# Window attention on one core: values' products in 64-row halves behind the scores, totals in the values' bank copied by ScalarE, TensorE's loop filled to whole fetch blocks

## The reference

```python
x = x + conv(_gn(x))
# conv: q, k, v = xh @ Wq, xh @ Wk, xh @ Wv ; split into 16 windows of 8 x 8
sim = einsum('bmhid,bmhjd->bmhij', q * scale, k) + pos_emb   # i, j: windows; m: place in the window
attn = softmax(sim)
o = einsum('bmhij,bmhjd->bmhid', attn, v) @ Wo + bo
```

## Time and profile before

| | us |
|---|---|
| median of 3 runs | 3674.86 (3674.0 to 3676.15) |
| the profiled execution | 3674.84 |
| its span in the profile | 3672.9 |
| TensorE busy | 3608.4 (98%) |
| VectorE busy | 3032.9 (83%) |
| ScalarE busy | 2940.0 (80%) |
| GpSimd busy | 2045.4 (56%) |

### The profile page before, as it was taken

One profiled execution on the slowest core, in us unless ns is written; L12 is line 12 of the kernel. 1 busy time (PEld: TensorE's weight loads), 2 busy tenths in 40 slices (PEclk: granted clock), 3 DMA queues, 4 the chain that ended last, 5 costly groups with the idle time before them and its releaser, 6 DMA issues.

```text
span 3672.9 us, 167555 instructions
## 1 busy us (share of the span) xinstructions
PE 3608.4 (98%) x67842; PEld 2625.2 (71%) x67842; DVE 3032.9 (83%) x5028; ACT 2940.0 (80%) x5377; POOL 2045.4 (56%) x3334
## 2 busy tenths in 40 slices
PE   5999999999999999999999999999999999999998
PEld 3777777777777777777777777777777777777776
DVE  6888888888888888888888888888888888888876
ACT  6888888888888888888888888888888888888874
POOL 4555555555555555555555555555555555555553
PEclk9999999999999999999999999999999999999999
DMA  4555555555555555555555555555555555555544
GB/s 95 139 144 136 146 144 142 137 145 143 141 138 150 142 137 143 145 143 137 143 146 144 136 145 144 144 134 145 143 145 135 145 142 145 136 146 143 141 126 117
DMA packets 252111, 513.67 MB, mean 140 GB/s; under 512 B 62672, under 2 KB 63120, under 8 KB 251536
## 3 DMA queue, kind: packets, MB, share of 16 engines
q1 hardware_dynamic: 250000, 504.35, 52.4%
q10 hardware_dynamic: 1536, 0.07, 0.0%
HBM read 118.31 MB, written 117.44 MB: 64 GB/s over the span
## 4 chain that ended last, share of the span: by engine, by line
PE 87%; issue 5%; POOL 3%; DVE 2%; ACT 1%; DMA 0%; POOLq 0%; SPq 0%; DVEq 0%; ACTq 0%
PE ps_out L327 18%; PE ps_q L327 16%; PE ps_k L327 16%; PE ps_v L327 14%; PE ps_o L370 13%; PE ps_s L358 10%; POOL sc L724 1%; ACT xn L484 1%; POOL xlo L732 1%; POOL newton L706 1%; DVE part L622 0%; POOL sc L737 0%; PE ps_tot L423 0%; DVE sc L651 0%; DVE pt_f L664 0%
## 5 line engine op out<-in xcount | busy, mean ns | idle before, releaser
L724 POOL TENSOR_TENSOR sc<-sc,mx 128x512 f32<-128x512 f32 x512 | 536.5, 1048 | 876.3 <-DVE mx L658 876.3
L484 ACT ACTIVATE xn<-x_sb,norm_add,norm_mul 112x128 f32<-112x128 f32 x2048 | 1016.7, 599 | 5.0 <-POOL norm_add L717 3.1
L737 POOL TENSOR_TENSOR sc<-sc,rs 128x512 f32<-128x512 f32 x512 | 536.4, 1048 | 421.7 <-DVE rs L678 421.6
L327 PE MATMUL ps_out<-ohi,wo_s 128*112 128x256 f16 x4096 | 720.8, 278 | 3.1 <-DVE x_sb L634 3.1
L646 DVE TENSOR_TENSOR olo<-ps_o,ohi 128x512 f16<-128x512 f32 x512 | 353.8, 691 | 350.0 <-ACT ohi L526 338.8
L511 ACT ACTIVATE sc<-sc 128x512 f32<-128x512 f32 x512 | 323.3, 632 | 396.3 <-POOL sc L724 396.1
L327 PE MATMUL ps_q<-xhi,wqk 112*128 112x512 f16 x2048 | 611.2, 380 | 12.5 <-POOL xlo L732 9.9
L327 PE MATMUL ps_k<-xhi,wqk 112*128 112x512 f16 x2048 | 609.7, 379 | 0.6 <-ACT q_sb L501 0.6
L370 PE MATMUL ps_o<-p_bd,v_sb 128*32 128x128 f32 x16384 | 553.5, 276 | 9.1 <-DMA p_bd<-pt_f 6.6
L327 PE MATMUL ps_v<-wv_s,xhi 112*128 112x224 f16 x4096 | 560.6, 259 | 0.0
L732 POOL TENSOR_TENSOR xlo<-xn,xhi 112x1024 f16<-112x1024 f32 x256 | 547.3, 2138 | 13.1 <-ACT xhi L495 13.1
(11 more groups left out here) (76 smaller groups left out, 5827.6 us busy)
## 6 DMA issues: line engine op xcount, KB each, us to landing
k_bd<-k_cut SPq DMA_DIRECT2D x1024, 128.0 KB
p_bd<-pt_f SPq DMA_DIRECT2D x2048, 64.0 KB, 2.5
x_sb<-in_x SPq DMA_DIRECT2D x256, 448.0 KB, 4.5
out_y<-x_sb SPq DMA_DIRECT2D x256, 448.0 KB, 3.5
k_cut<-in_L_conv_Wq SPq DMA_DIRECT2D x2, 98.0 KB
k_cut<-in_L_conv_Wk SPq DMA_DIRECT2D x2, 98.0 KB
k_cut<-in_L_conv_Wv SPq DMA_DIRECT2D x2, 98.0 KB
pt_f<-in_L_conv_Wo SPq DMA_DIRECT2D x8, 24.5 KB
```

The lines of the kernel that those rows point to most:

```text
L327: last = nc.tensor.matmul(dst, w_parts(a, ch), x_parts(c, ch), start=(n == 0), stop=(n == 3 * chunks - 1))
L484: nc.scalar.activation(xn[:, b % 2, :, c4, :, :, nw].rearrange("p r c q -> p q r c"), x_sb[:, b % XBUFS].rearrange("p ch (nh r w) -> p (ch ...
L724: nc.gpsimd.tensor_tensor(rows, rows, mx[:, t % 2].unsqueeze(2).broadcast_to(by_row), ALU.subtract).then_inc(shifted, 1)
L737: nc.gpsimd.tensor_tensor(rows, rows, rs[:, t % 2].unsqueeze(2).broadcast_to(by_row), ALU.mult).then_inc(probs, 1)
```

## The change

Seven things:

1. `weigh_values` makes 64 matmuls in place of 32: each takes 64 rows (half of the tokens) and 64 moving columns. The halves write different banks; ps_o has two banks now, laid out by place, unit and window, so an output is four runs of 16 columns, 128 columns apart. p_bd is half as wide. `in_x_order`, by which ohi and olo read ps_o, has a step of 128 columns over both banks where it was 16 in one.
2. The waits of the values' products move up to those of the scores, ahead of the last k matmul, and the products follow the scores with nothing between.
3. ps_tot has no bank of its own: it lies in the v projection's bank behind the values' columns. Its matmul moves from the end of the step to between the q and v projections of the next one (TOT_LEAD 12 to 11; the join stays where it was, as JOIN_LEAD 12).
4. ScalarE copies and scales the totals into st (`keep_means`), between keeping q and keeping v. VectorE's operation that did so is gone, STAT_OPS is 6.
5. VectorE's six remaining operations of the statistics stand in one run after the residual add.
6. In each step the first 3, 3 or 2 q matmuls after the first are cut in two of 256 columns, by `cut(t)`, 64 matmuls more in a round.
7. TensorE's loop starts at slot 66 of a fetch block of 256 instructions (`head_slot`).

```diff
-LOAD_LEAD, SUM_LEAD, RSQ_LEAD, TOT_LEAD, STAT_LEAD = 15, 14, 13, 12, 11
+LOAD_LEAD, SUM_LEAD, RSQ_LEAD, JOIN_LEAD, TOT_LEAD, STAT_LEAD = 15, 14, 13, 12, 11, 11
...
-        p_bd = sb("p_bd", [128, 2, PAIRS, UNIT * 32])
+        p_bd = sb("p_bd", [128, 2, 2, UNIT * 32])
...
-        ps_o = ps("ps_o", [128, UNIT * 32])
-        ps_tot = ps("ps_tot", [128, 2 * G])
+        ps_o = ps("ps_o", [128, 2, 512])
+
+        ps_tot = ps_v[0:CP, 0, C:C + 2 * G]
...
+        def cut(t):
+
+
+            return (3, 3, 2)[t % 3]
+
...
-            return ap.rearrange("p (u c n) -> p u n c", u=T2 * HG, n=WIN)
+
+            return ap.rearrange("p a (c u n) -> p u n (a c)", c=WS // 2, n=WIN)[:, 0:T2 * HG]
...
-                        last = nc.tensor.matmul(dst, w_parts(a, ch), x_parts(c, ch),
-                                                start=(n == 0), stop=(n == 3 * chunks - 1))
+                        for cols in (slice(0, HTOK // 2), slice(HTOK // 2, HTOK)) if 0 < n <= in_two else (slice(None),):
+                            last = nc.tensor.matmul(dst[:, cols], w_parts(a, ch), x_parts(c, ch)[:, cols],
+                                                    start=(n == 0), stop=(n == 3 * chunks - 1))
...
+            def total(b, i):
+                if b is None:
+                    return
+                per_image(pe, joined, b, i)
+                per_image(pe, means, b - 1, i)
+                nc.tensor.matmul(ps_tot, ones[0:CP, 0:CP], both[:, b % 2], start=True, stop=True).then_inc(totals, 1)
...
-                        for h in range(HPG):
-                            unit = (((h // 2) * T2 + t2) * HG + hg) * 2 + h % 2
-                            col = (t2 * HG + hg) * 128
-                            last = nc.tensor.matmul(
-                                ps_o[h * 32:h * 32 + 32, col:col + 128].rearrange("p (r j) -> p r j", j=32),
-                                v_sb[:, g % VBUFS, t2, hg * HPG + h, :],
-                                p_bd[:, g % 2, :, unit * 32:unit * 32 + 32], start=True, stop=True)
+                        for half in range(2):
+                            rows = slice(half * 64, half * 64 + 64)
+                            for h in range(HPG):
+                                unit = (((h // 2) * T2 + t2) * HG + hg) * 2 + h % 2
+                                products = ps_o[h * 32:h * 32 + 32, half, :].rearrange("p (c u n) -> p c u n", c=WS // 2, n=WIN)
+                                last = nc.tensor.matmul(
+                                    products[:, :, t2 * HG + hg, :],
+                                    v_sb[rows, g % VBUFS, t2, hg * HPG + h, :],
+                                    p_bd[rows, g % 2, :, unit * 32:unit * 32 + 32], start=True, stop=True)
...
-                    project_qk(u, 0).then_inc(q_done, 1)
+                    project_qk(u, 0, None, cut(t)).then_inc(q_done, 1)
                     per_step(pe, v_kept, u - 1, i)
+                    if image_at(t - 1, TOT_LEAD) is not None:
+                        per_image(pe, means, image_at(t - 1, TOT_LEAD), i)
+                    total(image_at(t, TOT_LEAD), i)
                     project_v(u).then_inc(v_done, 1)
                     per_step(pe, k_kept, u - 1, i)
-                    project_qk(u, 1, score_waits).then_inc(k_done, 1)
+                    project_qk(u, 1, attention_waits).then_inc(k_done, 1)
...
+            def keep_means(b, i):
...
+                per_image(act, totals, b, i)
+                per_image(act, factors_ready, b - 1, i, 2)
+                wait(act, stats, STAT_OPS * (b - 1) + 2, i, STAT_OPS * XBUFS)
+                nc.scalar.activation(st[:, :], ps_tot, ACT.Copy, scale=1.0 / GROUP_N).then_inc(means, 1)
...
+HEAD_SLOT = 66
```

More of the change, by code:

```diff
@@ L152, in build @@
         totals = sem("totals")
+        means = sem("means")
         stats = sem("stats")
@@ L182, in build @@
         final = sem("final")
-        STAT_OPS = 7
+        STAT_OPS = 6
         NEWTON = 3
@@ L195, in wait, with rounds @@
                 eng.wait_ge(s, n + i * per_round)
-        def rounds(eng, step, **prepare):
+        def cut(t):
+            return (3, 3, 2)[t % 3]
+        def rounds(eng, step, head_slot=None, **prepare):
             for t in range(FIRST, LOOP_AT):
@@ L202, in rounds @@
                 step(t, 0)
-            with nc.Fori(0, ROUNDS, engines=[eng.engine], hint_back_edge=True) as i:
+            with nc.Fori(0, ROUNDS, engines=[eng.engine], hint_back_edge=True, head_slot=head_slot) as i:
                 for t in range(LOOP_AT, LOOP_AT + PERIOD):
@@ L319, in _, with split_product @@
         def _(pe):
-            def split_product(dst, w_parts, x_parts, chunks=CH, waits=None):
+            def split_product(dst, w_parts, x_parts, chunks=CH, waits=None, in_two=0):
                 n = 0
@@ L333, in _, with project_qk @@
             o_parts = (ohi, olo)
-            def project_qk(u, j, waits=None):
+            def project_qk(u, j, waits=None, in_two=0):
                 h, hg = divmod(u, 2)
@@ L377, in step, with attention_waits @@
                 u = t + PROJ_LEAD
-                def score_waits():
+                def attention_waits():
+                    g = t - PV_LAG
+                    if is_step(g):
+                        probs_placed(pe, g, i)
+                        per_step(pe, v_kept, g, i)
+                        per_step(pe, o_lo, g - 1, i)
                     g = t + 1
@@ L418, in step @@
                     last.then_inc(projected, 1)
-                b = image_at(t, TOT_LEAD)
-                if b is not None:
-                    per_image(pe, joined, b, i)
-                    wait(pe, stats, STAT_OPS * (b - 1) + 1, i, STAT_OPS * XBUFS)
-                    nc.tensor.matmul(ps_tot[0:CP, :], ones[0:CP, 0:CP], both[:, b % 2],
-                                     start=True, stop=True).then_inc(totals, 1)
             def bound_weights():
@@ L436, in _ @@
             pe.wait_ge(zeroed, N_ZEROED)
-            rounds(pe, step, before_11=bound_weights, before_4=weights_split)
+            rounds(pe, step, {pe.engine: HEAD_SLOT}, before_10=bound_weights, before_4=weights_split)
         @block.scalar
@@ L586, in stat_op @@
                 if n == 0:
-                    per_image(dve, totals, b, i)
+                    per_image(dve, means, b, i)
                     per_image(dve, factors_ready, b - 1, i, 2)
@@ L644, in step @@
                     per_step(dve, o_hi, g, i)
-                    nc.vector.tensor_tensor(olo[:, g % 2], in_x_order(ps_o[:, :]), ohi[:, g % 2],
+                    nc.vector.tensor_tensor(olo[:, g % 2], in_x_order(ps_o[:, :, :]), ohi[:, g % 2],
                                             ALU.subtract).then_inc(o_lo, 1)
@@ L664, in step @@
                     nc.vector.transpose(pt_f[:, (t - 1) % 2], sc[:, (t - 1) % 2]).then_inc(turned, 1)
-                stat_op(stat_b, 3, i)
                 add_out(t - FINAL_LAG, i)
-                stat_op(stat_b, 4, i)
-                stat_op(stat_b, 5, i)
+                for n in range(STAT_OPS):
+                    stat_op(stat_b, n, i)
                 group_sums(image_at(t, SUM_LEAD), 0, i)
```

37 lines of the change are left out of this document (16 added, 21 removed).

## The result

The changed kernel takes 3865.3 us (median of 4 runs, 3849.5 to 3868.7) against 3674.7 before: ratio 1.051, interval 1.048 to 1.0539. It is 190.6 us slower. The prediction was 3666.5 in a range of 3657 to 3688: wrong in sign and size.

What follows compares the result with a forecast made beforehand. A ring of VectorE, GpSimd and ScalarE (28.17 us an image) was taken to bound, just above TensorE's 28.08. Ring -5.1, tail -3, last products -0.5 and filling +0.3 gave -8.3 from 3674.84: 3666.5 us, own range 3661 to 3672, overall 3657 to 3688.

Steps and rivals of the forecast that it cites:

- Loop of whole blocks: Placing TensorE's loop in whole instruction blocks: concerns only its instruction supply, TensorE has spare time, so 0.
- rival (d): 128 matmuls and loads in one stretch starve TensorE of instructions; decides above 0.2 us a step, about 3735 us; chance 0.06.
- the products' own term: Values' products on TensorE in 64 halves take 0.79 us at most instead of 1.01: gain taken as 0.22 a step.
- Waits joined: Products' waits moved before the last k matmul: TensorE stalls there, but with 2.3 us spare before ohi it costs nothing.
- the steady ring: Closed chain of row maximum, subtraction, exponential, ScalarE's list, ohi, olo, scores' bias, next maximum: 28.17 us an image.
- the ring's 5: Image laps of 28.12 us against 28.17 once TensorE is no longer behind: -5.1 us over 120 images, between 0 and -8.
- the tail's 3: In the last steps TensorE sets the pace, so its gain counts there: -3 us, between -1 and -4.
- two bounds of nearly equal length: The VectorE, GpSimd and ScalarE chain at 28.17 us an image and TensorE's own work at 28.08, the former in force.
- rival (b): ohi and olo read the new output layout more slowly; at 0.05 us each about 3717 us; chance 0.08.
- (c): Strided output over two banks slows the values' products to 2.02 us a step, about 4170 us; chance 0.04.
- lower bound of the new stretch: Shortest time expected for TensorE's values' products in halves: half of 1.01 us, a gain of 0.5 a step.
- Rival (a): TensorE is the real bound, so the products' gain carries through: -76 us, about 3598; chance 0.05.

Runs made afterwards that it cites:

- experiment 2: The changed kernel with the products' halves kept but without the cut q matmuls and the placed loop head: 3889.8 us, ratio 1.06 to the kernel before.
- experiment 3: The changed kernel with only the loop's head moved, from slot 66 to slot 24 of a block: 3911.2 us, one run.
- (6): The changed kernel with scores between v and k, products behind the output projection, and the loop's head at slot 0: 3779.9 us, ratio 1.0298 to the kernel before.
- (10): The kernel before with 64 more instructions a step, made by cutting long q, k and v matmuls into pieces, products as before: 3720.5 us, ratio 1.0119.
- experiment 9: The kernel before with each values' product of 128 columns cut into two of 64, still 128 rows, one bank and old waits: 3832.9 us, ratio 1.0428.
- experiments 1: The changed kernel with products over 128 rows again, no cut q matmuls and no placed head; joined waits, totals and statistics stay changed: 3685.9 us, ratio 1.0027.
- 8: The changed kernel with 128-row products, no cut q matmuls, no placed head, and the products' waits back behind the scores: 3674.6 us, ratio 0.9999 to the kernel before.
- experiment 5: The kernel before with one edit, ScalarE adding the bias to x ahead of the exponential instead of ahead of ohi: 3668.8 us, ratio 0.9983.

## Why the prediction was wrong

**The step that failed** is "Loop of whole blocks. It concerns TensorE's instruction supply alone; TensorE has the spare time, so 0", and rival (d) with it. The placing itself is not what costs (experiment 2); what failed is the reason given, that a TensorE with spare time cannot lack instructions, and the products' own term, which has no supply in it. I saw that 128 matmuls and their loads now stand in one stretch, asked whether TensorE starves by 0.2 a step, answered from "the scores issue 64 in 0.79 today" and gave it 0.06 and 3735. But 64 scores are 128 instructions, half a block; before, the next group was 32 long products. The change makes it 256 instructions in 1.41 us, a whole block in about the time of one packet (1.15). In the kernel after this costs some 16.6 us a round, clock included (178.9 - 162.3, an estimate): 0.69 a step, 3.5 times the 0.2 from which I had it decide. That TensorE waits for blocks is shown by the places (experiment 3) and by the packets that end 1.39 us before it goes on. That the dense stretch brings it about is shown by the 174 us of issue waits of the products that go when the same matmuls stand in another order (6), and by their absence with the number alone (10); experiment 9 adds stalls without the 64-row form, but most of them at the loop's turn. At that turn the kernel after loses 51 us in 19 turns, and how much of this is the last block of 66 instructions and how much the density stays open.

The rows of before had what was needed. There scores and products are 192 instructions in 1.80 us, and the 64 others of a block beside them stand for 3 to 4 us of long matmuls (24 of the output projection 1.45, 12 of q 1.29, 24 of v 1.15): some 5 us at the worst. I weighed the supply against a whole step and not against a block.

The Trainium skill (Runtime: NRT & Kernel Launch, Instruction fetch mechanics) says that instructions come in 16 KiB blocks of 256, fetched while the current one runs, and that crossing a boundary is "mostly hidden". The packets of 16 KB and the places agree with the first; this case disagrees with the second, by 0.7 to 3.2 us at the eight crossings of a round that fall late in the dense stretch (medians; 3.2 is from experiment 3), and not at the other 24, where nothing shows.

**The clock** was no term at all. After the stall of 2.90 us shown above the granted clock is at its lower level (1.2 GHz) for some us; over the kernel the mean is 0.983. Counted at full length, 0.017 x 3866 = 66 us of a clock not had, an upper bound since part of it lies in waits.

**Waits joined: "costs nothing"** was wrong by 10 us (experiments 1 and 8). The argument was made for the steady ring, where the two traces hardly part, and not for filling, for draining and for a DMA that comes late once.

**Sum and tail.** Neither the ring's 5 nor the tail's 3 could be seen: no run had the dense stretch without its stalls. The laps where nothing stalls (28.04 to 28.08) are those of the kernel before at the same place, so they test neither. The sum's one reading of the tail, that TensorE's gain counts there, is not shown by any run.

**Right**: two bounds of nearly equal length, with the ring the one in force (experiment 5: 3668.8, forecast 3660 to 3670); ohi and olo at the same cost, so rival (b) is out; the strided output without cost, so (c) is out, against the sentence of the Trainium skill (PSUM — Partial Sum Buffer) that I had weighed. The size of the halves' gain was low: 0.39 a step, not 0.22, and nearer my lower bound of the new stretch. Rival (a) needs TensorE alone as the bound; experiment 5 speaks against it, since a shorter ring alone gained 6 us.

## What to carry to other kernels

When a change adds short instructions to TensorE, count them in blocks of 256 and ask how long the shortest block runs, beside the time of one instruction packet: here a stretch of 256 in 1.41 us stalled in some 8 of 24 passes, where a block began late in it, by 0.7 to 2.9 us; one in 1.89 us (experiment 9) in one place of the round away from the loop's turn; and the same number of instructions spread over a step of 7 us in none. The last part of a loop's body is a block of its own: look how many instructions it holds. Join waits only of things that are needed together, and check filling and draining as well as the steady step.

## What the runs showed of the hardware

- A stalled boundary was crossed 1.39 us (median of 134 in the kernel after) after the end of a packet of instructions.
- TensorE stood at the loop's back edge 2.62 us where the loop ended 66 instructions into a block, and 0.1 where it ended 197 into one.
- 64-row products directly behind 64-row scores take 0.62, and both together 1.41; apart each takes 0.79. A projection behind either of them, or behind products of 128 rows, takes 0.11 to 0.16 more than behind another projection. Products of 128 rows cut from 128 to 64 columns cost 1.10 for 1.01.
- Four of six f16 matmuls of 512 columns in pieces of 128 cost 1.33 for 1.29.
- Outputs in runs of 16 columns, 128 apart over two banks, cost neither TensorE nor the engines that read them anything that shows: ohi and olo take 599 and 692 ns, 599 and 691 before.
